# A fused decoder layer on one core: the mixer's output projection as one stacked fp32r matmul per token tile, and the routing's counting matmuls in fp32r

## What is computed

```python
# 1 mixer: a small recurrence of 16 states, then its output projection
h  = silu(causal_conv4(x @ in_w.T + in_b))
xp = h @ xp_w.T + xp_b
a, b = exp(-exp(xp[..., :16])), silu(xp[..., 16:]) * h.sum(-1, keepdims=True)
ys = scan(state = state * a + b)              # over the 256 tokens
x  = layernorm(x + ys @ out_w.T + out_b)      # out_w is 256 x 16
# 2 cross attention: 8 heads of 128, keys are 77 context rows and the 256 tokens
x  = layernorm(x + attention(q=ln(x), kv=[ln(ctx), ln(x)]) @ Wo + bo)
# 3 mixture of 8 experts, top 2, capacity counted over the tokens in order
ones = (weights > 0); keep = cumsum(ones, axis=0) <= capacity
x  = layernorm(x + moe(x))
```

## Time and profile before

| | |
|---|---|
| median of 3 runs | 1152.58 us (1151.61 to 1152.69) |
| span of the profiled execution | 1152.0 us |
| PE busy | 1043.9 us, 91% |
| DVE busy | 811.2 us, 70% |
| ACT busy | 663.1 us, 58% |
| POOL busy | 509.1 us, 44% |
| granted TensorE clock, mean | 0.961 of full speed |

### The profile page before, as it was taken

The page is one execution under the profiler, slowest core; times in us unless marked ns, Lnnn a source line. Parts: engine busy times, 40 slices in busy tenths (PEclk is TensorE's granted clock), DMA queues, the critical chain, the costliest instruction groups (busy, mean ns, idle before and its releaser), DMA issues. The chain is left out here.

```text
span 1152.0 us, 23422 instructions
## 1 busy us (share of the span) xinstructions
PE 1043.9 (91%) x7026; PEld 957.6 (83%) x7026; DVE 811.2 (70%) x2048; ACT 663.1 (58%) x1689; POOL 509.1 (44%) x838
## 2 busy tenths in 40 slices
PE   5699999999999999999999999999999999389970
PEld 4589999898989898989898989898899989279860
DVE  4677878687868787777777777877687866245435
ACT  4466656565656565656565666666556555045535
POOL 1324263626353544444444444453536353524463
PEclk8799999999999999999999999999999999679995
DMA  9300000000000010000101010100010000246647
GB/s 309 104 13 11 22 29 23 32 22 29 22 27 27 15 36 14 27 23 20 33 20 32 19 32 22 32 19 32 22 31 20 11 19 11 83 110 176 173 48 298
DMA packets 36374, 59.00 MB, mean 51 GB/s; under 512 B 3746, under 2 KB 27140, under 8 KB 36228
## 3 DMA queue, kind: packets, MB, share of 16 engines
q1 hardware_dynamic: 28548, 44.51, 11.6%
q0 software_dynamic: 7680, 12.72, 4.9%
HBM read 31.33 MB, written 25.89 MB: 50 GB/s over the span
## 5 line engine op out<-in xcount | busy, mean ns | idle before, releaser
L1239 POOL TENSOR_SCALAR prob<-prob,rinv 128x333 f32<-128x333 f32 x256 | 142.8, 569 | 370.3 <-DVE rinv L1097 368.5
L455 PE MATMUL ps<-kv_lo,w_hi 128*128 128x256 f32 (+1 forms) x512 | 170.7, 333 | 2.7 <-DVE kv_lo L876 2.7
L798 ACT ACTIVATE prob<-ps,nmx 128x333 f32<-128x333 f32 x256 | 135.2, 536 | 42.5 <-DVE nmx L1089 42.0
L456 PE MATMUL ps<-kv_hi,w_lo 128*128 128x256 f32 (+1 forms) x512 | 154.3, 301 | 0.0
L457 PE MATMUL ps<-kv_hi,w_hi 128*128 128x256 f32 (+1 forms) x512 | 154.3, 301 | 0.0
L793 ACT ACTIVATE oT_hi<-ps 128x256 fp32r<-128x256 f32 x128 | 49.1, 384 | 170.6 <-PE ps L457 167.1
L876 DVE TENSOR_TENSOR pT_lo<-ps,pT_hi 128x512 fp32r<-128x512 f32 (+1 forms) x256 | 131.0, 550 | 3.0 <-ACT pT_hi L810 2.6
L482 PE MATMUL ps<-ident,prob 128*128 128x128 f32 (+1 forms) x768 | 127.3, 275 | 3.8 <-POOL prob L1239 2.3
L1089 DVE TENSOR_REDUCE nmx<-ps 128x2 f32<-128x666 f32 x128 | 108.1, 845 | 20.9 <-PE ps L457 20.3
L455 PE MATMUL ps<-pT_lo,v_hi 128*128 128x256 f32 (+1 forms) x384 | 108.8, 283 | 2.1 <-DVE pT_lo L876 1.1
L457 PE MATMUL ps<-pT_hi,v_hi 128*128 128x256 f32 (+1 forms) x384 | 108.3, 282 | 0.0
(11 more groups left out here) (186 smaller groups left out, 3084.3 us busy)
## 6 DMA issues: line engine op xcount, KB each, us to landing
raw<-in_W SPq DMA_DIRECT2D x16, 512.0 KB
slots<-initr SPq DMA_DIRECT2D x8, 520.0 KB, 9.7
xsl<-slots SPq DMA_DIRECT2D x8, 520.0 KB, 6.9
xts<-in_xT SPq DMA_DIRECT2D x16, 256.0 KB, 2.7
xs<-in_x SPq DMA_DIRECT2D x16, 256.0 KB, 2.8
accd<-xrow SPq DMA_DIRECT2D x16, 256.0 KB, 2.2
fx<-accd SPq DMA_DIRECT2D x8, 512.0 KB, 6.6
out<-fx SPq DMA_DIRECT2D x8, 512.0 KB, 2.6
```

What stands on the lines that cost most here:

```text
L455: pe.matmul(dst, hi1, lo2, start=first, stop=False, skip_group_check=True)
L456: pe.matmul(dst, lo1, hi2, start=False, stop=False, skip_group_check=True)
L798: act.activation(prob[:, h % 2, t, 0:KEYS], ps[:, S0 + t, 0:KEYS], ACT.Exp, bias=nmx[:, h % 2, t:t + 1], accum_out=rsum[:, h % 2, t:t + 1] ...
L1239: pool.tensor_scalar(prob[:, h % 2, t, 0:KEYS], prob[:, h % 2, t, 0:KEYS], rinv[:, h % 2, t:t + 1], 1.0, ALU.mult, ALU.mult).then_inc(norm ...
```

## The change

- `ys` loses its row of ones, and a new tile `ys_x` of 96 rows in fp32r holds three copies side by side: rows 0 to 16 the high part of the states and a row of ones, rows 32 to 47 the low part (`ys` minus its high part), rows 64 to 80 the high part again, with ones. `oww_x` holds the weight's high part at 0 and 32 and its low part at 64. One matmul over 96 rows then gives high x high, low x high and high x low.
- ACT writes the two copies of the high part at the end of slot 4, after waiting for the scan. DVE writes the low part in a new step at (4, "D"), `state_lo`, which waits for ACT's first copy and stands ahead of slot 5's `nmx`. PE's op waits for the second copy and for the low part.
- At the start DVE clears `oww` and `ys_x`; SP loads the weight three times, behind the eight weight pieces; DVE waits for these loads before body -1, then writes ones, the copy and the low part of the weight.
- The matrices `upper`, `ones`, `tot` and `seen` become fp32r, so that cum takes one instruction for each matmul. Values there are whole numbers.

```diff
-            for dst, src in ((v16, vec16), (oww, out_w), (bor, bo), (embt, emb)):
+            for dst, src in ((v16, vec16), (bor, bo), (embt, emb)):
                 sp.dma_start(dst[:], src).then_inc(small_ld, 16)
...
+            sp.wait_ge(oww_set, 1)
+            for row in (0, 32, 64):
+                sp.dma_start(oww[row:row + NST + 1, :], out_w).then_inc(oww_ld, 16)
             sp.wait_ge(initr_set, 2)
...
                     if at(bb, 0):
-                        pe.wait_ge(small_ld, 64)
-                    need(pe, ys_set, bb + 1)
+                        pe.wait_ge(owx_set, 4)
+                    need(pe, ysc_set, bb + 1)
+                    need(pe, ysl_set, bb + 1)
                     for t in range(NT):
-                        last = pe.matmul(g[:, t * D:(t + 1) * D], ys[:, t * P:(t + 1) * P], oww[:], start=True, stop=True)
+                        last = pe.matmul(g[:, t * D:(t + 1) * D], ys_x[:, t * P:(t + 1) * P], oww_x[:],
+                                         start=True, stop=True)
...
+                    if h == 4 and "nxt" in have:
+                        need(act, ys_set, b + 2)
+                        need(act, op_mm, b + 1)
+                        act.activation(ys_x[0:NST, :], ys[:], ACT.Copy).then_inc(ysh_set, 1)
+                        act.activation(ys_x[64:64 + NST, :], ys[:], ACT.Copy).then_inc(ysc_set, 1)
                     for c in SPLIT_AT[h] if at(b, -1) else ():
...
-                    need(dve, op_mm, bb)
-                    dve.tensor_tensor_scan(ys[0:NST, :], dec[:], inp[:], 0.0, ALU.mult, ALU.add).then_inc(ys_set, 1)
+                    need(dve, ysc_set, bb)
+                    dve.tensor_tensor_scan(ys[:], dec[:], inp[:], 0.0, ALU.mult, ALU.add).then_inc(ys_set, 1)
...
-            dve.memset(ys[:], 1.0)
+            dve.memset(oww[:], 0.0).then_inc(oww_set, 1)
+            dve.memset(ap(ys_x[:]), 0.0).then_inc(owx_set, 1)
...
-            dve.wait_ge(small_ld, 64)
+            dve.wait_ge(small_ld, 48)
             dve.wait_ge(const_set, 1)
+            dve.wait_ge(owx_set, 1)
+            dve.wait_ge(oww_ld, 48)
+            dve.memset(ap(ys_x[0:32, :]), 1.0)
+            dve.memset(ap(ys_x[64:96, :]), 1.0).then_inc(owx_set, 1)
+            dve.tensor_copy(oww_x[:], oww[:]).then_inc(owx_set, 1)
+            dve.wait_ge(owx_set, 3)
+            minus(oww_x[64:96, :], oww[64:96, :], oww_x[64:96, :]).then_inc(owx_set, 1)
...
+            def state_lo(b, par, *tile):
+                need(dve, ysh_set, b + 2)
+                minus(ys_x[32:32 + NST, :], ys[:], ys_x[0:NST, :]).then_inc(ysl_set, 1)
...
                 (4, "C"): [("nxt", context_hi)],
+                (4, "D"): [("nxt", state_lo)],
...
-        upper = s1("upper", [P, P])
-        ones = s1("ones", [P, P])
+        upper = s1("upper", [P, P], F32R)
+        ones = s1("ones", [P, P], F32R)
...
-        tot = s1("tot", [P, NT, E])
-        seen = s1("seen", [P, NT, E])
+        tot = s1("tot", [P, NT, E], F32R)
+        seen = s1("seen", [P, NT, E], F32R)
```

More of the change, by code:

```diff
@@ L130, in build @@
         xpw = s1("xpw", [P, NC, 80])
-        oww = s1("oww", [NST + 1, D])
+        oww = s1("oww", [96, D])
+        oww_x = s1("oww_x", [96, D], F32R)
         vec = s1("vec", [P, V_N])
@@ L168, in build @@
         inp = s1("inp", [NST, S])
-        ys = s1("ys", [NST + 1, S])
+        ys = s1("ys", [NST, S])
+        ys_x = s1("ys_x", [96, S], F32R)
         xa = s1("xa", [P, NT, D])
@@ L250, in build @@
         passed, bq_set = sem("passed"), sem("bq_set")
+        oww_ld, oww_set, owx_set, ysh_set, ysl_set, ysc_set = (
+            sem("oww_ld"), sem("oww_set"), sem("owx_set"), sem("ysh_set"), sem("ysl_set"), sem("ysc_set"))
         s_mm, nmx_set, exp_set, rinv_set, norm_set = (
@@ L623, in body @@
                         pe.wait_ge(bvb_set, 1)
-                        pe.wait_ge(small_ld, 64)
+                        pe.wait_ge(small_ld, 48)
                         for g in range(H):
@@ L629, in body @@
                                       start=g == 0, stop=False)
-                        pe.matmul(ps[:, AVB, 0:D], ones[0:1, :], bor[:], start=False, stop=True).then_inc(cvec_mm, 1)
+                        pe.matmul(ps[:, AVB, 0:D], ap(ones[0:1, :]), bor[:], start=False, stop=True).then_inc(cvec_mm, 1)
                     if prev2:
@@ L780, in _ @@
             act.wait_ge(bq_set, 1)
-            act.wait_ge(small_ld, 64)
+            act.wait_ge(small_ld, 48)
             act.wait_ge(zero_set, 1)
@@ L1204, in _ @@
             pool.memset(ident[:], 0.0).then_inc(route_step, 1)
-            pool.memset(upper[:], 1.0).then_inc(route_step, 1)
-            pool.memset(ones[:], 1.0)
+            pool.memset(ap(upper[:]), 1.0).then_inc(route_step, 1)
+            pool.memset(ap(ones[:]), 1.0)
             pool.memset(powm[:], -0.5)
-            pool.memset(seen[:], 0.0)
+            pool.memset(ap(seen[:]), 0.0)
             pool.memset(initr[:], 0.0).then_inc(initr_set, 1)
@@ L1216, in _ @@
                                pattern=[[-1, P]], channel_multiplier=1)
-            pool.affine_select(out=upper[:], in_=upper[:], compare_op=ALU.is_ge, fill=0.0, base=0,
+            pool.affine_select(out=upper[:], in_=ap(upper[:]), compare_op=ALU.is_ge, fill=0.0, base=0,
                                pattern=[[1, P]], channel_multiplier=-1).then_inc(const_set, 1)
@@ L1292, in body @@
                         need(pool, seen_set, 2 * b - 2)
[L1293 removed]
+                        pool.tensor_tensor(seen[:, 1, :], ap(seen[:, 0, :]), ap(tot[:, 0, :]), ALU.add).then_inc(seen_set, 1)
                         pool.tensor_copy(xrow[:, :, D], tokf[:])
@@ L1303, in body @@
                         need(pool, seen_set, 2 * b - 1)
-                        pool.tensor_tensor(seen[:, 0, :], seen[:, 1, :], tot[:, 1, :], ALU.add).then_inc(seen_set, 1)
+                        pool.tensor_tensor(seen[:, 0, :], ap(seen[:, 1, :]), ap(tot[:, 1, :]), ALU.add).then_inc(seen_set, 1)
                         need_apart(pool, rank_set, b)
```

1 line of the change is left out of this document (removed).

## The result

| | before | after |
|---|---|---|
| median, runs on the same chip | 1152.37 us | 1179.12 us (1178.17 to 1179.74) |
| ratio | | 1.0228 (95% interval 1.0215 to 1.0240) |
| span of the profiled execution | 1152.0 us | 1176.4 us |
| PE busy | 1043.9 us, 91% | 1035.1 us, 88% |
| granted TensorE clock, mean | 0.961 | 0.950 |

What follows compares the result with a forecast made beforehand. DVE's chain from scan to ln (10.43 us) was taken as the bound there, not busy PE. Span 1152.0 + 13.0 start + 12.0 scan delay - 3.8 counting = 1173.2, plus 0.6 to the median: 1174 us, range 1161 to 1182.

Steps and rivals of the forecast that it cites:

- The start: Before the first attention: weight loads land at 20.8 us behind the pieces, making it 13.0 us later, ends 11.8 and 15.
- The delay behind the scan: DVE, scan to nmx: ACT's copy and the subtraction add 0.8 us in batches 1 to 15, 12.0 us in all.
- Neither end moves ln, so I count 0: Output projection op on PE: some 0.8 us shorter a batch, but covered by DVE's chain, so 0 and not 12 us.
- The counting: cum on PE, behind the chain: fp32r saves 0.24 us in each of 16 batches, 3.8 us less, ends 1.6 and 5.6.
- The chain itself: DVE from the scan's start through nmx, rinv, xa and lnp to ln: one chain of 10.43 us; PE bounds after ln.
- Rival D: PE's clock falls in the longer wait at ln: 1.7 us lost each batch, 1199 us in all; chance 6%.
- The price of 1.7 us: Time lost on PE to one clock fall, from 937 to 944 us at granted clock 0.76, applied to each batch.
- the sum: Whole profiled span: 1152.0 + 13.0 + 12.0 - 3.8 = 1173.2 us, before the step to the median.
- The last step, from span to median: Whole kernel: 0.6 us added to the 1173.2 us span gives a median of 1173.8, say 1174 us.
- one wait of 2.29 us: PE's idle time at 939.19 in the kernel before, which went with a clock fall to 1.2 GHz, 1.7 us lost.

## Why the prediction was right

The forecast was 1174 us, in a range of 1161 to 1182; measured are 1179.12 us. Its step by step:

- **The start: right, 0.8 us too small.** First tap 22.8 forecast, 23.22 measured; first w_lo 2.4 us behind the scan, 2.69 measured; first ln 13.0 us later, 13.76 measured. The loads ended at 21.0 (DVE goes on at 21.04), between the two values of the prediction, 20.8 and, by the estimate from the Trainium skill's page, 21.8 us. With the loads moved alone, 11.6 us go at the first ln. The last weight piece, issued at 8.45, landed 11.0 us later, at 19.5, so the landing behind the pieces is what DVE waited for, as forecast. What I hadn't foreseen is the issue: it took 4.17 us on SP behind the pieces, but it was over at 13.64, long before that landing, and can hardly have cost anything by itself; no run separates the two. The Trainium skill, page "DMA: Bandwidth & Descriptors", section on why a DMA increments its semaphore by 16, gave one engine for 17 rows and so an estimate of 1.9 us for the three; by the measured end it can't be told from a spread over more engines.
- **The delay behind the scan: right in mechanism, 12% too small.** 0.90 us a body, not 0.8. ACT's copy starts 0.71 us behind the scan's start as forecast, 0.45 us instead of 0.43 to DVE's subtraction, and this takes 0.45 us to nmx instead of 0.38: nmx doesn't overlap its end. Undoing it alone took 0.71 us of the 0.90 off; the spare scan in the kernel before shows that any delay there is paid.
- **"Neither end moves ln, so I count 0": right.** A projection four times as long and one on unchanged engines both leave the bodies as they are. dots waits for k_lo's bank, 0.93 us, as said.
- **The counting: right.** 0.47 to 0.24 us, 3.8 us forecast, 3.1 us measured alone.
- **The chain itself: half right.** The prediction followed it from the scan to lnp and took lnp and ln for its end, with PE as the bound behind them. The orders of DVE show that it goes on through k_lo of slot 6 and passes through every nmx; lnp is a branch beside it. cum, which the prediction placed where PE is the bound, starts when POOL's seen is there. The number came out all the same, because a delay ahead of nmx moves both.
- **Rival D, that the clock falls: true in part, and given 6%.** It falls in six of the 14 bodies, behind the wait at dots, and once behind a loop turn; windows of 10 us show 0.83 to 0.94. The price of 1.7 us that I took is near for the one behind the turn, 1.3 us; a body with slow passes behind dots reaches ln with less to wait and loses 0.2 to 0.5 us. Together it is 3.3 us. With the low part alone behind nmx the falls are gone (with the loads early too, one behind a turn is left), and the 14 bodies are 12.64 us shorter, of which the chain is 14 x 0.71 = 9.9 us and the loop's turns 0.5 us; taken as that difference, 2.2 us remain for the clock.
- **Not in the sum at all: the loop's turns.** PE's idle time "issue" went from 6.9 to 8.9 us in the six turns; from one start to the next it is 8.6 and 10.5 us. Of the 5.4 us left over above, 1.9 us are this and 3.3 us the clock (2.2 us by the difference), so that 0.2 to 1.3 us stay unexplained. Why a turn costs 0.9 us in one and 2.0 us in another is open: the kernels here have their own values, and the one with more matmuls has a second such gap.
- **The last step, from span to median, was mis-sized.** I added 0.6 us. In each kernel measured since, the profiled run took 1.7 to 1.8 us more than its span, and here it was the fastest of four, 0.95 us under their median. 24.4 us between the spans became 26.8 between the medians.
- **Two stretches came out shorter, unasked:** 1.45 us behind the first ln and 2.74 us from xp of batch 15 to the end. The last one varies between 245.4 and 248.5 us over all these kernels, though the stages behind it have the same code in all; I found no step of a kernel that goes with it. It is also why differences of 1 to 2 us between two medians here aren't read as the effect of an edit.

Added up against 1173.2 us of the sum: the start 0.8, the chain in the 14 bodies 1.4, the counting there 0.1, what was left over 5.4, less 1.45 and less 3.1 at the end (2.74, where the sum had 0.3 more) make the 3.2 us to the span of 1176.4; 2.1 us come from the last step. That the 5.4 us which the sum doesn't have and the 4.5 us that went missing elsewhere nearly cancel is luck: without those 4.5 us the time would have been some 1183.6 us, just outside the range.

## What to carry to other kernels

An operation that shortens the busiest engine is worth what its neighbours on the chain let through: find the engine whose queue has no gap, and price an added step by where it stands in that queue, not by its own 0.4 us. The step that a wait names need not be on the chain that is paid for; moving that step alone tells. And a small load belongs ahead of the large ones in its queue: the same three loads held the first tap back by 11.6 us behind eight pieces of 512 KB and by 0.04 us ahead of them.

## What the runs showed of the hardware

- The issue of three small loads took 4.17 us on SP behind eight pieces of 512 KB (2.97 us for the slowest of the three), and 0.93 us ahead of them.
- An idle time of 0.90 to 0.93 us ahead of dots, whose eight instructions have 8 columns each, was followed by a fall of the granted clock to 1.2 GHz in six of 14 bodies of the changed kernel, in three of 14 with the loads early, and by none in the others, with the same rows. One of 1.29 us ahead of ln was followed by none, and where the idle time at dots was 0.2 us (filled by matmuls, or with the low part behind nmx) no body had a fall behind it. What tells the bodies with a fall from the others stays open. The prediction had taken its measure from one wait of 2.29 us.
- Of the 84 turns of the hardware loop in all kernels here, the five with 1.77 to 1.95 us of idle time were each followed by a fall, and the others, with up to 1.74 us, by none. Such a fall cost 1.3 to 1.5 us, where one behind dots cost 0.1 to 0.5 us at cum, with ln's wait shorter instead.
- POOL's copy of 16x256 took 3.47 us beside DVE's w_lo and 0.39 us elsewhere; its power of four columns took 1.96 us beside w_lo and 1.04 us in the steady body. The Trainium skill, page "SBUF — State Buffer", section "SBUF: two separate sides", says that VectorE and GpSimd share one pair of ports, that a VectorE operation with two inputs in SBUF, as w_lo has, can hold it as an exclusive lock, and that the other engine then blocks fully. The trace fits: the copy ended 0.25 us behind the last of three w_lo in a row. No run here takes the ports apart from other causes. With the three parts moved to DVE, right behind the scan, the first ln came 1.7 us sooner. A step moved to an idle POOL isn't free where DVE streams large tiles.
- A turn of the hardware loop with two bodies cost PE 0.9 to 2.0 us of idle time ahead of the scores in these kernels, and 0.5 to 0.8 us more at a second place in the one with six more matmuls a body.
